# The first group of an expert loop: table 2 ahead of the pair's rows, the second expert's silu and the rows' copy ahead of the exponentials

## The reference

```python
xn = layernorm(x)
# attention, per head: q, k = elu(..) + 1;  S = k^T q;  out = (v S) / (sum(q * k) + 1e-6)
# y = xn + out @ Wo + bo;  attention = gamma * (y - mean) * rsqrt(var + 1e-3) + beta
gates = softmax(xn @ wg.T);  w_topk, idx_topk = top_k(gates, 8);  w_topk /= sum(w_topk)
buf[e, rank] = xn[token]                       # rank < 160
h = buf @ expert_w1[e].T;  x1, x2 = split(h)
y = (x1 * silu(x2)) @ expert_w2[e].T
moe = shared(xn) + scatter_add(token, y * w)   # shared: the same unit with its own weights
out = x + attention + moe
```

## Time and profile before

| | |
|---|---|
| median of 3 runs | 338.61 us |
| lowest, highest | 338.55, 343.72 us |
| profiled execution, its own time | 339.84 us |
| span of its instructions | 338.0 us |
| instructions | 9266 |
| granted TensorE clock, mean over the span | 0.999 of full |

### The profile page before, as it was taken

One profiled execution on the slowest core, in us unless ns is written; L12 is line 12 of the kernel. 1 busy time (PEld: TensorE's weight loads), 2 busy tenths in 40 slices (PEclk: granted clock), 3 DMA queues, 4 the chain that ended last, 5 costly groups with the idle time before them and its releaser, 6 DMA issues.

```text
span 338.0 us, 9266 instructions
## 1 busy us (share of the span) xinstructions
PE 321.0 (95%) x3059; PEld 306.3 (91%) x3059; DVE 262.8 (78%) x1071; ACT 206.4 (61%) x450; POOL 253.8 (75%) x258
## 2 busy tenths in 40 slices
PE   8999998799999999999999999999999999899964
PEld 8888787699999999999999899999999999899963
DVE  5789987797778778797978797788878776955476
ACT  4889925456666595747486857565686657554210
POOL 6887767357888778778877888787888888878563
PEclk9999999999999999999999999999999999999999
DMA  6999644599888879788888888888977797944788
GB/s 189 355 371 352 165 106 142 199 283 315 197 188 209 237 157 239 173 235 174 228 184 218 176 221 174 226 204 217 201 196 197 184 234 179 247 45 39 163 356 245
DMA packets 60126, 71.15 MB, mean 211 GB/s; under 512 B 14896, under 2 KB 47920, under 8 KB 60080
## 3 DMA queue, kind: packets, MB, share of 16 engines
q1 hardware_dynamic: 42736, 56.47, 53.9%
q0 software_dynamic: 15360, 13.12, 24.9%
q10 hardware_dynamic: 1984, 0.98, 1.0%
HBM read 54.72 MB, written 15.43 MB: 208 GB/s over the span
## 4 chain that ended last, share of the span: by engine, by line
PE 65%; ACT 11%; DVE 11%; issue 6%; DMA 4%; POOL 2%; SPq 0%; DVEq 0%; ACTq 0%; POOLq 0%
PE bank L1430 24%; PE bank L1440 10%; PE bank L1349 7%; PE bank L1363 4%; ACT L590 3%; PE bank L1477 3%; DMA ew<-acc 3%; PE bank L1449 2%; PE bank L1501 2%; PE bank L1522 2%; POOL acc L545 2%; PE bank L1396 2%; ACT L703 2%; PE bank L1517 1%; PE bank L1294 1%
## 5 line engine op out<-in xcount | busy, mean ns | idle before, releaser
L545 POOL DMA_INDIRECT acc<-ys,idx_g x64 | 102.3, 1599 | 26.0 <-issue 15.8
L1430 PE MATMUL bank<-xe,ew 128*128 128x160 f32 x768 | 116.0, 300 | 1.7 <-ACT xe L643 0.9
L1430 PEld LDWEIGHTS bank<-xe,ew 128*128 128x128 f32 x768 | 108.4, 190 | 4.3 <-ACT xe L643 1.5
L526 POOL DMA_INDIRECT gath<-xng,idx_g x80 | 81.5, 1019 | 30.5 <-issue 19.2
L618 ACT ACTIVATE si<-bank 128x480 f32<-128x480 f32 (+1 forms) x96 | 52.0, 541 | 60.9 <-PE bank L1430 35.0
L844 DVE TENSOR_TENSOR ac<-si,bank 128x480 f32<-128x480 f32 x64 | 41.7, 651 | 23.5 <-ACT si L618 21.9
L1440 PE MATMUL bank<-ew,ac 128*128 128x128 f32 x384 | 54.9, 279 | 0.0
L1349 PE MATMUL bank<-xT,shw 128*128 128x128 f32 x384 | 50.0, 278 | 0.0
L1440 PEld LDWEIGHTS bank<-ew,ac 128*128 128x128 f32 x384 | 48.3, 191 | 0.8 <-issue 0.2
L1349 PEld LDWEIGHTS bank<-xT,shw 128*128 128x128 f32 x384 | 46.5, 192 | 0.4 <-ACT cum L743 0.2
L1363 PE MATMUL bank<-shw,acs 128*128 128x128 f32 x192 | 27.7, 281 | 4.8 <-DVE acs L835 3.8
(11 more groups left out here) (169 smaller groups left out, 564.9 us busy)
## 6 DMA issues: line engine op xcount, KB each, us to landing
ew<-in_expert_w SPq DMA_DIRECT2D x64, 384.0 KB, 3.8
ew<-in_expert_w SPq DMA_DIRECT2D x64, 192.0 KB, 3.7
ew<-acc SPq DMA_DIRECT2D x8, 512.0 KB, 9.2
xng<-xn SPq DMA_DIRECT2D x8, 256.0 KB, 5.2
acc<-zeros SPq DMA_DIRECT2D x4, 512.0 KB, 5.4
acc<-betas SPq DMA_DIRECT2D x4, 512.0 KB, 3.8
x_sb<-in_x SPq DMA_DIRECT2D x7, 256.0 KB, 6.7
gath<-xng,idx_g POOLq DMA_INDIRECT x80, 3.7
```

The lines of the kernel that those rows point to most:

```text
L526: pool.indirect_dma_start(out=gath[:, p, m, :], out_offset=None, in_=xng, in_offset=bass.IndirectOffsetOnAxis(ap=idx_g[:, g % 5, m:m + 1], ...
L545: pool.indirect_dma_start(out=acc[adds_to[g, m]], out_offset=bass.IndirectOffsetOnAxis(ap=idx, axis=0), in_=src, in_offset=None, compute_o ...
L1430: last = pe.matmul(h_view(n, half_ + 1, CAP)[:, c, :], ew[p][m][:, k * P:(k + 1) * P], xe[:, p, m, :], start=True, stop=True)
```

## The change

Only orders change; no instruction is added or removed. On TensorE `table(2)` moves from behind `pair_rows(0)` to behind `queries_keys(1)`, and `keys_queries(1)` from ahead of `down(0,0)` to behind `down(0,1)`. On ScalarE the order of group 0 becomes silu(0,0), second_copy, narrow_copy(2), silu(0,1), pair_copy, load_exp, y_copy(0,0), exp_of(1), values_copy(1), load_silu, silu(0,2). On VectorE table_compare(2), table_tokens(2), expert_mul(0,1) and table_hot(3) stand ahead of features(1). The list of the uses of X follows. In all later groups the order is the old one.

```diff
--- before.py
+++ after.py
@@ -65,7 +65,7 @@
     q_uses = [('logits', r) for r in range(NR)]
     v_uses = [('first counts',)]
     for g in range(NG):
-        x_uses += [('pair', g)] + [('table', 2)] * (g == 0) + [('table', g + 3)] * (g + 3 < NG) + [('first', g + 1)] * (g + 1 < NG)
+        x_uses += [('table', 2)] * (g == 0) + [('pair', g)] + [('table', g + 3)] * (g + 3 < NG) + [('first', g + 1)] * (g + 1 < NG)
         a_uses += [('rest', g - 1), ('sum', g - 1)] * (g > 0) + [('table', 2)] * (g == 0) + [('same', g)] + [('table', g + 3)] * (g + 3 < NG)
         q_uses += [('qk', g)] * (g > 0) + [('out', g), ('project', g)]
         v_uses += [('values', g), ('kq', g), ('out T', g)]
@@ -755,21 +755,24 @@
                 silu(('e', g, 0))
                 if g == 0:
                     second_copy()
+                    narrow_copy(2)
+                    silu(('e', g, 1))
+                    pair_copy(g)
                 if attend:
                     load_exp()
                 if g > 0:
                     y_copy(g - 1, 3)
+                else:
+                    y_copy(g, 0)
                 if attend:
                     exp_of(g + 1)
                     values_copy(g + 1)
                     load_silu()
-                pair_copy(g)
-                silu(('e', g, 1))
-                if g == 0:
-                    narrow_copy(2)
                 if g > 0:
+                    pair_copy(g)
+                    silu(('e', g, 1))
                     rest_copy(g - 1)
-                y_copy(g, 0)
+                    y_copy(g, 0)
                 silu(('e', g, 2))
                 if g > 0:
                     sum_copy(g - 1)
@@ -1172,16 +1175,14 @@
                     shared_add4(4)
                 if a < B:
                     queries_keys(a)
-                if 0 < g < NG - 3:
+                if g == 0:
+                    table_compare(2)
+                    table_tokens(2)
+                    expert_mul(g, 1)
+                if g < NG - 3:
                     table_hot(g + 3)
                 if a < B:
                     features(a)
-                if g == 0:
-
-                    expert_mul(g, 1)
-                    table_compare(2)
-                    table_tokens(2)
-                    table_hot(3)
                 if a < B:
                     qk_product(a)
                     qk_sum(a)
@@ -1583,20 +1584,23 @@
                     down(g - 1, 3)
                 if a < B:
                     queries_keys(a)
+                if g == 0:
+                    table(2)
+                if a < B:
                     values(a)
                 up(g, 1)
                 pair_rows(g)
-                if g == 0:
-                    table(2)
                 if g > 0:
                     down_rest(g - 1)
-                if a < B:
-                    keys_queries(a)
+                    if a < B:
+                        keys_queries(a)
                 down(g, 0)
                 up(g, 2)
                 if g > 0:
                     rest_sum(g - 1)
                 down(g, 1)
+                if g == 0:
+                    keys_queries(a)
                 if g == NG - 1:
                     rest_turn(g)
                 elif g in unit:
```

## The result

The changed kernel takes 337.69 us, the median of 20 runs (336.0 to 340.74), against 340.48 for the kernel before over its 20 runs (337.7 to 345.03). The ratio is 0.9926, 95% interval 0.9903 to 0.9949: 2.5 us gained, between 1.7 and 3.3. That is within 2%. Some runs of a kernel lie several us above its others; the times given here are medians of all runs, the ratios and their intervals come from those within 1.5% of the kernel's fastest. The forecast gain of 3.8 us lies outside the interval, the 1.8 us of rival 1 inside.

The account below looks back on a forecast made before the run. The prediction took TensorE and a saturated GpSimd as two parallel chains, GpSimd carrying the end. Profiled 339.84 less the 3.8 us gain gave 336.0, less 1.23 to the runs' median 334.8 us; range 333.6 to 337.6.

Parts of the forecast that it names:

- rival 1: TensorE alone sets the end: gain only 1.8 us, time 336.8 us; chance 0.17.
- TensorE, right: Group 0, idle time before table 2 removed: up(0,2) 2.8 us earlier, 1.8 us kept from up(0,3) on.
- The two new stalls: TensorE in group 0 waits for features(1) and for silu(0,2), 0.6 us each.
- ScalarE, right: Group 0: y_copy(0,0) at 60.85, silu(0,2) from 63.64; 1.40 us from table load to next useful activation.
- VectorE, right: Work moved ahead of features(1) ends at 61.6, before the exponential at 61.9, so it is covered.
- GpSimd's first scatters: Scatters (0,0) to (0,3): with the same landings, GpSimd reaches its saturated stretch 3.8 us earlier.
- The step that failed: From 79.29 on GpSimd keeps its own pace, so all 3.8 us reach the accumulator loads.
- Rival 2: Slower, scatters meet the weights: a 1.07 us wait in each of 12 groups, about 347.6 us; chance 0.08.
- The tail: Accumulator loads start at 311.5 instead of 315.30, first add without wait, second load last; end moves by 3.8 us.
- The level: Median of the runs before taken as 338.61 us, 1.23 below the profiled execution, giving 334.8 us.

Follow-up runs that it names:

- the four traces of the faster kind: Profiles on the faster chips: kernel before, changed kernel, changed with GpSimd memsets before scatter (0,3), changed with accumulators exchanged; deciding-set ratios of the last two: 0.9945, 0.9894.
- the swap: Changed kernel with the two accumulators exchanged, so scatter (0,1) need not wait for (0,0)'s landing: 0.9972, 0.9942 and 0.9894 of the kernel before.
- the delay on GpSimd: Changed kernel with four memsets, 3.7 us as planned, on GpSimd ahead of scatter (0,3): 1.0014, 1.0001, 1.0016 and 0.9945 of the kernel before.
- the deciding set: Changed kernel with GpSimd memsets ahead of scatter (0,3), 0.9945, and with accumulators exchanged, 0.9894, against the kernel before at 341.37 us.

## Why the prediction was right and wrong

**TensorE, right.** The sum put up(0,2) 2.8 us earlier and up(0,3) 1.8. Against the first expert's product they moved by 3.91 - 0.92 = 2.99 and 2.77 - 0.92 = 1.85. The two new stalls were 0.38 and 0.45 us, forecast at 0.6 each, at the places named. Every later group up to 13 keeps 1.80 to 1.85.

**ScalarE, right.** y_copy(0,0) was due at 60.85 and stands at 59.91 + 0.92 = 60.83; silu(0,2) was due at 63.64 and stands at 62.66 + 0.92 = 63.58. From a table load to the next useful activation it is again 59.91 - 58.51 = 1.40 us, and 62.66 - 61.26 = 1.40.

The Trainium skill's ScalarE: Activation LUTs (What ACT_TABLE_LOAD costs) would have had a drain of some 1.38 us on top of the load. The trace after disagrees as that of before did: only the 1.28 of the load is there.

**VectorE, right.** What moved ahead of the features stayed covered, save that they came late by the 0.38 us above.

**GpSimd's first scatters, nearly right.** Forecast 3.8 us earlier at (0,3), measured 3.6 without the 0.92. The wait of (0,1) for the first landing stayed 6.3 us from its start (67.41 - 61.07), that of (0,3) became 7.4.

**The step that failed** is the one after it: "So from 79.29 on, no scatter waits for the expert computation; GpSimd goes at its own pace", and from it "all 3.8 us pass through to the accumulator loads". That no scatter waits for its data is true in both traces. That its pace is its own is not. The trailing of 4 to 9 us was read as slack that could be spent once. In the rows of all sixteen groups it was not level: it climbs from 4.17 at (1,0) to 7.03 at (13,0). Over the four traces of the faster kind GpSimd's way from (1,0) to (13,0) is the longer the less it trails (195.3 us from 4.96, 199.3 from 0.78), and that is where the gain went: 3.6 us at (0,3), 2.3 at the accumulator load. From (0,3) to (15,4) the changed kernel's GpSimd needs 235.79 us where before needed 234.49. Its 142 transfers ahead of (15,4) are busy for 189.94 against 188.51 us, while the waits, by what they have beyond the 0.30 us, hold 2.5 against 2.75. So the 1.3 us went into longer transfers, not into waits. With the swap there are both, 189.72 us busy and 4.8 of waits, and 237.87 in all. That the transfers are longer because they meet the weights' at this distance is my reading of it; no run took the weights' transfers away, and it stays open.

**The rivals.** Rival 1, TensorE alone, came nearest: 1.8 us, measured 2.5 (1.7 to 3.3), and the load at the end moved by 315.30 - 312.06 = 3.24, or 2.3 without the 0.92. It was dismissed for the 2.91 us and more by which scatters trail, which is no evidence of a pace of their own. That it came nearest does not show it: the load moved by 0.5 us more than TensorE did, and the delay on GpSimd was not without effect on the load. Rival 2 saw that less distance could cost GpSimd time, and had the form and the size wrong: no more waits for landings but longer transfers, 1.3 us over the whole way, not 1.07 in each of 12 groups.

Perfetto Trace Analysis of the Trainium skill (Identifying the Most-Contended Engine) picks the engine with the highest occupancy, here TensorE at 96% beside GpSimd's 77%. The prediction set that aside; the times of the run that holds GpSimd back agree with the rule (0.6 us lost of 2.5), its trace only up to group 13.

**The tail, right as a mover, wrong in its details.** The sum had the first add start without a wait and the second load come last. In the trace VectorE waits 1.79 us for the first load, but not for the second: the third add follows at 321.40 with no long wait, where it had waited until 325.65. From the first load to the end it takes 334.2 - 312.06 = 22.1 us, 22.7 before.

**The level.** Even with the right ratio, 0.9926 x 338.61 = 336.1, the measured 337.69 would have been missed by 1.6 us. Of the 2.9 us between 334.8 and 337.69, 1.9 are the level and 1.0 the gain that fell short, which by the medians is 2.8. The median of three runs of before was 0.55% low, as much as the difference in dispute.

## What to carry to other kernels

An engine that trails another without waiting for it is not thereby a bound with its own pace: look at how the distance runs from group to group. If it settles on one value from any start, a head start of the trailing engine is worth little or nothing. A delay of it is another matter: look for the buffers that the leading engines take back from it, since through these it can hold them up, as at the start of group 15 here. For a gain of 1% compare the two profiles from the last common point ahead of the change, and take the level of before from more than three runs.

## What the runs showed of the hardware

The kernel before takes about 340 us in the result's runs and on the chip of the deciding set, and 353 to 358 on three other chips, with the granted clock at 1.00 in the windows of both kinds shown. On the latter the weights' transfers land in a median of 7.7 to 9.1 us against 3.6 to 3.9, TensorE stops now and then for some 0.4 us within a run of like loads, and the gain of this change is between nothing and 1%. Whether the gain itself differs between the two kinds can't be told from the noise.

GpSimd's queue of gathers and scatters, with a least gap of 0.30 us, behaves like a follower in the four traces of the faster kind: started 0.8, 2.5, 4.2 or 5.0 us behind its data, it trails by 7.0 to 7.2 twelve groups later. When it trails by 9.72 us at (13,2), ScalarE waits 1.84 us for a landing, at 9.27 us 0.39. Where groups last some 17 us in place of 15.9 it trails by about 2.
